# Attention steps of a fused attention and feed-forward kernel: the second normalisation moves from VectorE to ScalarE, and GpSimd works out a bias for it

## The reference

```python
x = x + xattn(layernorm(x), ctx)          # 16 heads, q and k normalised per head
x = x + ffn(layernorm(x))                 # the second normalisation
def layernorm(x, eps=1e-5):
    m, v = mean(x), var(x)                # over the 128 features of a token
    return (x - m) / sqrt(v + eps)
```

## Time and profile before

| | us |
|---|---|
| median of 3 runs | 222.16 (221.98 to 222.17) |
| the profiled execution, its own time | 221.93 |
| its span, first to last instruction | 220.0 |
| attention steps 0 to 14, from the first exponentials to the last parts copied | about 26 to 123 |
| the stretch of 10 steps from 39.46 to 105.57 | 66.11, so 6.61 a step |
| feed-forward network | about 125 to 220 |

### The profile page before, as it was taken

One profiled execution on the slowest core, in us unless ns is written; L12 is line 12 of the kernel. 1 busy time (PEld: TensorE's weight loads), 2 busy tenths in 40 slices (PEclk: granted clock), 3 DMA queues, 4 the chain that ended last, 5 costly groups with the idle time before them and its releaser, 6 DMA issues.

```text
span 220.0 us, 8369 instructions
## 1 busy us (share of the span) xinstructions
PE 186.6 (85%) x3308; PEld 145.8 (66%) x3308; DVE 186.0 (85%) x344; ACT 147.8 (67%) x228; POOL 118.7 (54%) x168
## 2 busy tenths in 40 slices
PE   1277899999999999999987789429999999987784
PEld 0166778888888888888876545218676566764673
DVE  6634758999999899999999648699799999999992
ACT  2021678877778877778877577748688887887421
POOL 7335558667677667687762332034455644456440
PEclk9999999999999999999999999975999999999589
DMA  3372011111011111000000000000011010110103
GB/s 100 89 206 58 21 32 55 51 51 50 25 34 51 51 48 39 23 10 24 3 3 9 3 3 0 0 0 0 12 38 48 0 51 1 50 48 0 51 0 95
DMA packets 14829, 7.86 MB, mean 36 GB/s; under 512 B 1072, under 2 KB 14576, under 8 KB 14800
## 3 DMA queue, kind: packets, MB, share of 16 engines
q1 hardware_dynamic: 14272, 7.20, 11.7%
q10 hardware_dynamic: 528, 0.25, 0.4%
HBM read 5.35 MB, written 2.10 MB: 34 GB/s over the span
## 4 chain that ended last, share of the span: by engine, by line
PE 49%; DVE 22%; issue 11%; POOL 10%; ACT 3%; DMA 2%; SPq 1%; DVEq 0%; POOLq 0%; ACTq 0%
PE bank_o L1012 7%; PE banks_p L982 7%; POOL y_raw L406 5%; PE banks_p L954 5%; PE banks_s L996 5%; DVE banks_p L841 4%; PE bank_o L1022 4%; DVE frac L834 4%; PE banks_p L964 3%; PE banks_s L1119 3%; DVE y_raw L849 3%; DVE act_q L855 3%; PE banks_p L950 2%; PE bank_o L1134 2%; DMA bkv_rep<-in_L_xattn_bkv_dram 2%
## 5 line engine op out<-in xcount | busy, mean ns | idle before, releaser
L406 POOL TENSOR_TENSOR y_raw<-g_lo,y_raw 128x1024 f32<-128x1024 f32 x15 | 35.4, 2363 | 38.7 <-DVE frac L834 37.9
L1134 PEld LDWEIGHTS bank_o<-w,act_q 128*128 128x128 f32 x224 | 30.8, 216 | 5.5 <-DVE act_q L855 4.7
L460 ACT ACTIVATE probs<-banks_s 128x512 f32<-128x512 f32 x64 | 33.0, 609 | 0.9 <-PE banks_s L996 0.9
L1134 PE MATMUL bank_o<-w,act_q 128*128 128x128 f32 x224 | 31.9, 302 | 0.5 <-DVE act_q L855 0.3
L334 POOL TENSOR_TENSOR parts<-qk_hat,parts 128x512 f16<-128x512 f32 x16 | 18.6, 1162 | 23.9 <-DVE parts L644 23.9
L1119 PE MATMUL banks_s<-x2T,w 128*128 128x512 f32 x60 | 30.9, 596 | 0.0
L530 ACT ACTIVATE banks_p<-seg,gelu_hi 128x1024 f32<-128x1024 f32 x16 | 17.9, 1118 | 9.3 <-DVE y_raw L849 9.3
L521 ACT ACTIVATE g_lo<-seg,gelu_lo 128x1024 f32<-128x1024 f32 x16 | 18.4, 1149 | 6.3 <-DVE seg L828 6.3
L982 PE MATMUL banks_p<-ident,parts 128*128 128x128 f16 x256 | 20.1, 222 | 2.9 <-POOL parts L334 1.8
L1012 PE MATMUL bank_o<-probs,v_blk 128*32 128x64 f32 x1024 | 20.7, 222 | 1.0 <-DVE attn L675 1.0
L620 DVE TENSOR_SCALAR xn_all<-x_all,stats,rstd 128x128 f32<-128x128 f32 (+1 forms) x32 | 20.2, 670 | 1.1 <-POOL rstd L328 1.1
(11 more groups left out here) (113 smaller groups left out, 426.1 us busy)
## 6 DMA issues: line engine op xcount, KB each, us to landing
x_all<-in_x_dram SPq DMA_DIRECT2D x16, 128.0 KB, 2.5
c_in<-in_ctx_dram SPq DMA_DIRECT2D x16, 128.0 KB, 2.2
out_dram<-x_all SPq DMA_DIRECT2D x7, 256.0 KB, 2.3
w<-in_L_ffn_w_dram SPq DMA_DIRECT2D x2, 256.0 KB, 3.4
out_dram<-x_all SPq DMA_DIRECT2D x2, 128.0 KB, 1.9
b_rows<-in_L_ffn_b_dram SPq DMA_DIRECT2D x1, 192.0 KB, 3.5
wkv_raw<-in_L_xattn_Wkv_dram ACTq DMA_DIRECT2D x1, 128.0 KB, 3.0
bkv_rep<-in_L_xattn_bkv_dram SPq DMA_DIRECT2D x1, 128.0 KB, 5.2
```

The source lines that it names most:

```text
L406: g.tensor_tensor(y_raw[u][:], g_lo[n % 3][:], y_raw[u][:], ALU.add).then_inc(S[f"gelu{u}_done"], 1)
L460: a.activation(probs[i][:].rearrange("p t g n -> p (t g n)"), bank_s(i), ACT.Exp).then_inc(S["probs_ready"], 1)
L1134: last = t_.matmul(out, act_q[u][:, c, P * t:P * t + P], w2[:, CH // UNITS * u + c, :], start=False, stop=(u == UNITS - 1 and t == GT - 1 ...
```

## The change

VectorE's two `norm_x2` instructions of each step, (x - mean) * rstd, are taken away for steps 0 to 12 and given to ScalarE, as two activations `Identity(scale * x + bias)` whose scale and bias are columns of one value per row. They stand behind the four exponentials of step s and do the normalisation of step s-2. GpSimd gets two more instructions in `rstd_x2`: the product mean * rstd, and its subtraction from zero, which gives the bias. For steps 13 to 15 the normalisation stays on VectorE. One small constant is set once by GpSimd.

```diff
             g.memset(minus_half[:], -0.5).then_inc(S["consts_set"], 1)
-            pool.wait_ge(S["consts_set"], 2)
+            g.memset(zeros[:], 0.0).then_inc(S["consts_set"], 1)
+            pool.wait_ge(S["consts_set"], 3)
...
                 g.tensor_tensor(rstd2[:], var_eps2[:], minus_half[:], ALU.pow).then_inc(S["ln2_rstd"], 1)
+                if not isinstance(s, int) or s < STEPS - 3:
+                    pool.wait_ge(S["ln2_rstd"], s + 1)
+                    g.tensor_tensor(shift2[:], stats2[:, :, 1], rstd2[:], ALU.mult).then_inc(S["ln2_shift"], 1)
+                    pool.wait_ge(S["ln2_shift"], s + 1)
+                    g.tensor_tensor(bias2[:], zeros[:], shift2[:], ALU.subtract).then_inc(S["ln2_bias"], 1)
...
+            def norm_x2(s):
+
+                wait(act, "ln2_bias", s + 1)
+                for t in range(2):
+                    a.activation(xn2_all[:, tok(s, t, 2)], x_all[:, tok(s, t, 2)], ACT.Identity, bias=bias2[:, t:t + 1],
+                                 scale=rstd2[:, t:t + 1]).then_inc(S["xn2_ready"], 1)
...
                     for i in range(4):
                         exps(s, i)
+                if runs(s - 2, STEPS):
+                    norm_x2(s - 2)
...
                     heads_out(s - 1)
-                if runs(s - 2, STEPS):
+                if isinstance(s, int) and s == STEPS - 1:
                     norm_x2(s - 2)
```

More of the change, by code:

```diff
@@ L134, in xattn_ffn @@
         rstd2 = sb("rstd2", [P, 2])
+        zeros = sb("zeros", [P, 2])
+        shift2 = sb("shift2", [P, 2])
+        bias2 = sb("bias2", [P, 2])
         xn2_all = sb("xn2_all", [P, TOKENS])
@@ L203, in xattn_ffn @@
             g_qk g_squared g_ms g_logged g_rms g_normed  g_high g_parts_t g_parts_copied g_scores g_max
-            ln2_stats ln2_var ln2_rstd xn2_ready x2_t x2_t_copied h_first hz_first h_proj hz_ready
+            ln2_stats ln2_var ln2_rstd ln2_shift ln2_bias xn2_ready x2_t x2_t_copied h_first hz_first h_proj hz_ready
             seg_ready frac_ready glo_ready ghi_ready rise_ready slope_done gelu0_done gelu1_done actq0_ready actq1_ready
```

## The result

The changed kernel takes 225.38 us (median of 4 runs, 225.07 to 226.81) against 222.16 of the kernel before: a ratio of 1.015, interval 1.010 to 1.020. It is slower by 3.2 us; 4.5 had been forecast. Its profiled execution takes 225.07 us with a span of 223.2, 3.2 above the 220.0 of before, so the two traces can be compared piece by piece.

The account below looks back on a forecast made before the run. A closed loop of exponentials, squares, parts' copy and second transposes, meeting TensorE's of nearly equal length, was taken as the bound. 11 x 0.77 - 3.1 = 5.4, less 0.9 relief, gave +4.5 us: 226.6 us, range 224.0 to 228.2.

Parts of the forecast that it names:

- The closed row of exponentials, squares, parts' copy and second transposes: ScalarE to TensorE in a normal step: a gapless loop as long as the step, lengthened by the pair about 0.5 us.
- The rival that VectorE paces the steps: Ten attention steps: relieving VectorE lets steps fall to TensorE's busy 65.17 us, gaining 0.9, time 220.4 us; chance 0.08.
- The pair's price: ScalarE's queue behind the exponentials: the two activations cost 0.77 us a step, 0.385 each, both columns costing the same.
- the lower bound of 0.60: ScalarE's pair if the scale column is free: 0.60 us a step, +2.6 us in all, 224.8 us.
- The cover: Steps 2 to 12 on ScalarE: slack that hides 3.1 us of the eleven pairs, in three parts.
- The overlap with the last exponential: ScalarE, steps 2 to 12: the pair can overlap the last exponential, 0.10 us a step, 1.1 in all.
- VectorE's relief: Steps 13 and 12, where VectorE carries the bias parts: gains of 0.7 and 0.2 us, together 0.9.
- The wait for the bias: ScalarE, ahead of the queued squares: bias ready over 1.5 us before the exponentials end, so it costs nothing.
- the idle time ahead of the squares: ScalarE between exponentials and squares, steps 2 to 12: idle time covering 1.4 us of the pairs.
- the late copies: ScalarE's parts' copy, sometimes waiting for TensorE's first transposes: 0.6 us of cover over eleven steps.
- the rival in which those stalls cover nothing: TensorE's stalls fall elsewhere in the step: +5.7 us, 227.9; chance 0.12 together with the pair not overlapping at all.
- the one in which vanishing stalls take up more of the delay: Gains meet the cost: pair between 0.36 and 0.45 us, or vanishing TensorE stalls absorb delay; 222.2 to 223 us; chance 0.06.

Follow-up runs that it names:

- The pair twice: Changed kernel with ScalarE's pair issued twice, the first into a spare tile: 234.39 us, ratio 1.059 to the kernel before.
- without its column: Changed kernel with the scale column left out of ScalarE's pair, bias column kept: 224.3 us, ratio 1.012 to the kernel before.
- the pair at another place: Changed kernel with ScalarE's pair between the RMS norm's Exp and the copy of outT, one step later: 220.54 us, repeated 220.65.
- the removed instructions: Kernel before without the second normalisation of steps 0 to 12 on any engine: 221.07 us, ratio 0.997.
- the second traces: Both kernels run again unaltered: the changed kernel 225.98 us, ratio 1.021; the kernel before 221.71 us, ratio 1.0004.
- GpSimd's instructions alone: Kernel before plus GpSimd's product and subtraction in steps 0 to 12, bias unread, run twice: ratios 1.0063 and 1.0028 to the kernel before.

## Why the prediction was right, and where it was off

- **What bounds the kernel.** The closed row of exponentials, squares, parts' copy and second transposes was the right reading. The pair twice (0.75 a step for 0.77) and without its column (0.195 for 0.18) show that the step follows that row one to one, and the pair at another place that nothing else in the change counts in these steps. The wait was forecast at one spot and came at two: TensorE stops for the squares ahead of the V projection, and only for what is left of the delay for the parts' copy. The rival that VectorE paces the steps fell with the removed instructions: 0.06 a step, and nearly nothing in seven of ten.
- **The pair's price.** 0.77 us was taken and 0.77 measured; the lower bound of 0.60 is out, since the second column costs 90 ns. That it fits to the hundredth is luck: one activation takes 0.519 instead of 0.485, and it overlaps the next by 0.13 instead of 0.10, and the two errors cancel.
- **The cover.** From the exponentials of step 2 to those of step 13 the trace grew by 77.31 - 72.48 = 4.83 us; 5.4 was forecast, so the eleven pairs found 3.6 us of cover and not 3.1. This is the term that was mis-sized. The overlap with the last exponential was taken as 0.10 a step. Measured, the pair starts at 69.05, where the exponentials end at 69.20: 0.15. That makes 0.55 over eleven steps, the size of the difference. Adding up the pieces of the eleven steps in both traces bears it out: from exponentials to squares +5.35 (forecast 8.47 - 1.4 - 1.1 = 5.97), from squares to the parts' copy -0.75 (forecast -0.6), from that copy to the next exponentials +0.23 (forecast nothing). In the second traces the eleven steps grew by 4.97.
- **VectorE's relief.** Forecast 0.7 in step 13 and 0.2 in step 12, both of which fall between the exponentials of steps 13 and 14. Measured, 13 to 14 fell from 7.29 to 6.32, 0.97. Against the second trace of the kernel before, which lacks TensorE's stall of 0.62, it is 0.78. The gain stands, since the kernels that only remove VectorE's pair or place ScalarE's pair elsewhere have 6.35 and 6.40. But with both of VectorE's and of ScalarE's pairs in place it is 6.68, 0.4 to 0.6 less as well: with TensorE waiting each step, part of VectorE's lateness is hidden, so not all of the 0.97 is relief. Nor does it come the way that was forecast, as 0.92 us taken out of a row. From `heads_out` to the mean square VectorE takes 2.94 us instead of 3.02 in the first trace of the kernel before and 3.29 in the second, because the bias instructions that follow became 0.81 us longer (last section); the larger part is that `heads_out` begins 0.44 behind the exponentials of step 13 instead of 1.34 or 0.87. From the mean square to the exponentials of step 14 it is 2.93 or 2.94 in each of these traces.
- **The rest of the sum.** The forecast of 4.5 us came out as 3.2 and, on another chip, as 4.5 (225.98 against 221.50), so the medians don't say by how much the sum was off; the pieces do. Of the 3.2 us that the span grew, the eleven steps give +4.83 and 13 to 14 -0.97. The stretch ahead of the exponentials of step 2 gives -0.46 (39.00 against 39.46) and the stretch behind those of step 14 -0.20. Neither was forecast, and neither belongs to the change: in the traces here the exponentials of step 2 start between 38.36 and 40.03, whatever the kernel, and in two of one kernel at 39.00 and 39.25.
- **GpSimd.** 0.54 forecast, 0.55 measured, with 1.0 to 1.4 us of room left in steps 2 to 13. The wait for the bias never showed. The price holds only because the bias doesn't meet VectorE's cast of the parts here: in the second trace with GpSimd's instructions alone the subtraction takes 0.53 to 0.74 in six steps. The room covered that too.
- **What was said of a normal step** (7.0 to 7.15 us, activations of about 0.48, VectorE idle for about 1 us before the mean square, TensorE waiting some 0.5) came out as 7.04 to 7.13, 0.52, 1.76, and 0.37 for the squares with 0.14 for the copy: VectorE's idle time was too low, because the squares themselves came 0.6 later, and TensorE's wait for the copy alone is 0.3 by its weight loads, not 0.5.

TensorE's irregular stalls are gone in the changed kernel (steps 3 to 10 take 7.04 to 7.13, where before they ran from 6.49 to 7.03), taken up by the new wait. The forecast had counted on that: of the cover, the idle time ahead of the squares came to 1.47 (1.4 forecast) and the late copies to 0.75 (0.6). So the rival in which those stalls cover nothing is out, and the one in which vanishing stalls take up more of the delay got no more than the forecast had given it.

## What to carry to other kernels

An engine with a fifth of its time free is not free everywhere: ask which of its instructions close a row with the engine that sets the pace, and put moved work into the idle time that the profile shows in brackets, not behind a burst because it is convenient. Here the same two activations cost 5 us behind the exponentials and nothing 2 us later in the step. The price of such a move is the moved instruction's time in the queue, minus what the row has of real slack, times the steps, and a doubled or shortened copy of it measures that directly.

## What the runs showed of the hardware

Some instructions of VectorE and GpSimd lengthen each other when they run at once, and a removed instruction then only hands that on to its neighbour. Step 13's stretch in the changed kernel, VectorE and then GpSimd in order of time:

```profile
117.47 1.19 DVE L748 TENSOR_TENSOR b_rest<-b_rows,b_parts 64x640 f32<-64x640 f32 x1
118.70 0.91 DVE L750 CAST b_parts<-b_rest 64x640 f16<-64x640 f32 x1
...
116.83 1.16 POOL L343 TENSOR_TENSOR parts<-qk_hat,parts 128x512 f16<-128x512 f32 x1 [1.24 <-DVE parts L662]
117.95 1.31 POOL L350 TENSOR_TENSOR x_all<-x_all,attn 128x256 f32<-128x256 f32 x1
```

In the kernel before, where VectorE's normalising pair ran beside GpSimd's residual and these two came after it:

```profile
114.94 0.81 DVE L730 TENSOR_TENSOR b_rest<-b_rows,b_parts 64x640 f32<-64x640 f32 x1
115.78 0.48 DVE L732 CAST b_parts<-b_rest 64x640 f16<-64x640 f32 x1
...
114.17 0.76 POOL L341 TENSOR_TENSOR x_all<-x_all,attn 128x256 f32<-128x256 f32 x1
```

The same subtraction takes 1.19 instead of 0.81, the cast 0.91 instead of 0.48, the residual 1.31 instead of 0.76: 1.36 us more on the two engines after an instruction pair of 1.0 was removed. Which one suffers is a matter of order, as the same stretch shows in the kernel with only two normalisations on ScalarE:

```profile
111.45 0.69 DVE L662 CAST parts<-qk_hat 128x1024 f16<-128x1024 f32 x1
113.36 0.81 DVE L748 TENSOR_TENSOR b_rest<-b_rows,b_parts 64x640 f32<-64x640 f32 x1
114.20 0.90 DVE L750 CAST b_parts<-b_rest 64x640 f16<-64x640 f32 x1
...
111.46 0.73 POOL L337 TENSOR_TENSOR bias<-zeros,shift 128x2 f32<-128x2 f32 x1
113.52 1.23 POOL L350 TENSOR_TENSOR x_all<-x_all,attn 128x256 f32<-128x256 f32 x1
```

Here the subtraction starts ahead of the residual and takes its 0.81 although they overlap for 0.65 us; it is the residual, second to start, that takes 1.23 instead of 0.73. In all these rows the instruction that starts first keeps its time, and the second grows by 0.13 to 0.15 less than what the first still had to run: the subtraction by 0.38 (0.52 of `lows` left), the residual by 0.58 (0.71 of the subtraction left; it takes 0.73 alone), the cast by 0.43 (0.56 of the residual left), GpSimd's bias by 0.53 (0.68 of the cast left). Not all instructions do this: the same bias takes 0.20 beside VectorE's `normalise`, which reads PSUM. The Trainium skill (GPSIMD Engine Reference, Key points) says that GpSimd shares its SBUF interfaces with VectorE and names instructions in a two-port mode or with two SBUF inputs as those that contend; these rows agree for the subtraction, which has two SBUF inputs.

TensorE's clock between 120 and 130 us is not a matter of the kernel alone: of two traces of the changed kernel one was granted 1.00 and one 0.72 from 124 to 130, and the same piece of program took 7.25 and 8.20 us. In both TensorE had stood for 1.46 us before, waiting for `lows`, and so it had in both traces of the kernel before, whose clock stayed at 1.00. Executions of one kernel lie 1 us and more apart here; how much of that is this clock, no run shows.
